# Packing the halves of Q and K without a DRAM buffer, and masks that stay on chip

## The reference

```python
def _L0_attn_ref(x, W_qkv, W_out, b_out):      # 16 heads of 32, WINDOW = 128
    qkv = jnp.einsum('ble,ef->blf', x, W_qkv).reshape(b, l, 16, 32, 3)
    q, k, v = ...                               # heads first
    q = q * cos + _rotate_half(q) * sin         # RoPE on neighbouring pairs
    k = k * cos + _rotate_half(k) * sin
    mask = (j <= i) & (j >= i - WINDOW)
    scores = jnp.where(mask, q @ k.T * 32 ** -0.5, finfo.min)
    out = softmax(scores) @ v
    return out.reshape(b, l, e) @ W_out + b_out

x = x + _layernorm(_L0_attn_ref(_layernorm(x), W_qkv, W_out, b_out))
x = x + _layernorm(_L0_ffn_ref(_layernorm(x), W_up, W_gate, W_down))   # ternary weights, SwiGLU, 512 -> 2048 -> 512
```

## Time and profile before

| what | us |
|---|---|
| median of 3 runs | 1574.02 (1569.62 to 1575.28) |
| the profiled execution, its own time | 1572.07 |
| its span, first to last instruction | 1570.3 |
| PE busy / DVE busy over the span | 1337.6 / 1078.8 |
| ACT busy / POOL busy over the span | 725.6 / 497.0 |
| first and last masking on DVE start at | 54.9 and 777.2 |

### The profile page before, as it was taken

The page is one execution under the profiler, slowest core; times in us unless marked ns, Lnnn a source line. Parts: engine busy times, 40 slices in busy tenths (PEclk is TensorE's granted clock), DMA queues, the critical chain, the costliest instruction groups (busy, mean ns, idle before and its releaser), DMA issues. The chain is left out here.

```text
span 1570.3 us, 23805 instructions
## 1 busy us (share of the span) xinstructions
PE 1337.6 (85%) x7942; PEld 732.5 (47%) x7942; DVE 1078.8 (69%) x2567; ACT 725.6 (46%) x1410; POOL 497.0 (32%) x594
## 2 busy tenths in 40 slices
PE   3678979988897897888540799999999999999995
PEld 2355646555564655555320344444444444444442
DVE  3678979888897888889729545646465555556553
ACT  1465766667666666756535223232322323232321
POOL 2535664655656456565320000102010101101011
PEclk9888989999998999999675899999999999999998
DMA  9588889889898879889834000000000000000000
GB/s 349 143 176 173 169 194 178 160 184 187 167 171 189 178 155 189 171 169 179 160 139 184 0 1 0 28 1 28 0 28 1 0 28 0 28 1 28 1 28 27
DMA packets 363769, 164.62 MB, mean 105 GB/s; under 512 B 293632, under 2 KB 348160, under 8 KB 362624
## 3 DMA queue, kind: packets, MB, share of 16 engines
q1 hardware_dynamic: 363648, 163.11, 46.1%
HBM read 64.42 MB, written 25.17 MB: 57 GB/s over the span
## 5 line engine op out<-in xcount | busy, mean ns | idle before, releaser
L587 ACT ACTIVATE prob<-prob,peak 128x256 f32<-128x256 f32 x512 | 230.6, 498 | 180.1 <-DVE peak L709 178.9
L883 PE MATMUL J<-xnT,weights 128*128 128x512 f32 x512 | 257.9, 630 | 7.9 <-ACT xnT L571 7.9
L709 DVE CUSTOM_DVE_ANT_0 prob<-S,band,neg_score_scale 128x256 f32<-128x256 f32 x512 | 226.4, 479 | 35.1 <-DMA band<-in_bands 23.8
L1127 DVE SCALAR_TENSOR_TENSOR su<-U,sig 128x512 f32<-128x512 f32 x128 | 88.5, 692 | 198.6 <-ACT sig L1063 196.8
L718 DVE SCALAR_TENSOR_TENSOR parts<-prob,parts 128x512 f16<-128x512 f32 x256 | 209.8, 820 | 19.3 <-ACT parts L595 19.1
L1063 ACT ACTIVATE sig<-U,sig_scale 128x512 f32<-128x512 f32 x128 | 88.1, 688 | 231.3 <-PE U L1205 231.3
L1205 PE MATMUL U<-xT_hi,up_q 128*128 128x512 f16 x512 | 194.6, 380 | 0.0
L1205 PE MATMUL U<-xT_lo,up_q 128*128 128x512 f16 x512 | 194.6, 380 | 0.0
L1216 PE MATMUL Y<-down_q,h_hi 128*128 128x512 fp8e4 x512 | 194.1, 379 | 0.5 <-DVE h_lo L1138 0.5
L1205 PE MATMUL G<-xT_hi,gate_q 128*128 128x512 f16 x512 | 194.0, 379 | 0.0
L1205 PE MATMUL G<-xT_lo,gate_q 128*128 128x512 f16 x512 | 194.0, 379 | 0.0
(11 more groups left out here) (122 smaller groups left out, 1980.6 us busy)
## 6 DMA issues: line engine op xcount, KB each, us to landing
spill<-split SPq DMA_DIRECT2D x64, 256.0 KB, 2.6
Qp<-spill SPq DMA_DIRECT2D x128, 128.0 KB, 2.8
Kp<-spill SPq DMA_DIRECT2D x128, 128.0 KB, 2.9
out_x<-o_sb SPq DMA_DIRECT2D x8, 1024.0 KB, 4.3
X<-in_x SPq DMA_DIRECT2D x1, 6144.0 KB, 25.7
weights<-parts SPq DMA_TRANSPOSE x256, 3.2
Kc<-Kp SPq DMA_DIRECT2D x32, 128.0 KB, 3.0
w_gate_here<-in_w_gate SPq DMA_DIRECT2D x2, 2048.0 KB, 9.7
```

The lines of the kernel that those rows point to most:

```text
L587: e = nc.scalar.activation(prob[:, u % 4, h, :], prob[:, u % 4, h, :], ACT.Exp, bias=peak[:, u % 4, h:h + 1], scale=-1.0)
L709: e = nc.vector.tensor_tensor_reduce(out=prob[:, u % 4, h, :], in0=S_ps[u % 2][:, h * 2 * P:(h + 1) * 2 * P], in1=(band0 if first_tile els ...
L883: e = pe.matmul(dst[:], W[:, s, c, g * P:(g + 1) * P], xnT[:, c, :], start=(c == 0), stop=(c == DC - 1))
L1127: nc.vector.scalar_tensor_tensor(su[:, c % 2, :], U_ps[c % 2][:], H_SCALE / XN_SCALE ** 2, sig[:, c % 2, :], ALU.mult, ALU.mult).then_inc( ...
```

## The change

- `spill_q`, `spill_k`, the DRAM buffer and its two semaphores go. `pack_q` and `pack_k` now read `split` in SBUF directly and wait for what the spill waited for (`r_lo_done`), beside their own waits. Their numbers, sizes and targets stay: four DMAs of 128 KB for each group.
- For that the rows of a group are in another order: dimension by dimension with the head innermost (row = 4 x dimension + head). The 128 rows of `split`, read in order, are then the 32 rows of a pack's target with four heads in each. The columns of the Q and K weights and the rows of the RoPE tables are permuted on the host, and the shuffle swaps rows 4 apart instead of 1.
- `moves` is shortened: packs stand at units 0 (K1), 5 (Q2), 6 (K2), 16 (Q3), 18 (K3), 24 (next Q0), 25 (next K0), 30 (next Q1). Before they stood at 1, 5, 8, 17, 19, 25, 26 and 31.
- `rotated_high` waits for the packs of the group before (64 for each group) where it waited for the spill (16).
- `band0` is loaded once and kept; `logits` takes it only for the first query tile of a batch and `band` otherwise. The load at unit 28 and its wait go; DVE waits once for it before its first work.

```diff
-        spill = nc.dram_tensor("spill", [2, 2, P, MT], F16).ap()
-            def spill_q(i, g):
-                n = i * NG + g
-                q_split, packed_before = worked_out(sp, 2 * n + 1, 64 * n)
-                sp.wait_ge(r_lo_done, q_split)
-                at_least(sp, q_packed, packed_before)
-                sp.dma_start(spill[0].rearrange("s p t -> p s t"), split[:, 0]).then_inc(q_spilled, 16)
             def pack_q(i, g):
                 n = i * NG + g
-                written, scored = worked_out(sp, 16 * (n + 1), (n - 1) * STEPS)
-                sp.wait_ge(q_spilled, written)
+                q_split, scored = worked_out(sp, 2 * n + 1, (n - 1) * STEPS)
+                sp.wait_ge(r_lo_done, q_split)
                 at_least(sp, score_done, scored)
                 for row, part in enumerate((0, 0, 1, 1)):
-                    sp.dma_start(Qp[row * HD:(row + 1) * HD, g % 2],
-                                 spill[0, part].rearrange("(h d) t -> d h t", h=4)).then_inc(q_packed, 16)
+                    sp.dma_start(Qp[row * HD:(row + 1) * HD, g % 2], split[:, 0, part]).then_inc(q_packed, 16)
...
-            moves = {0: [(spill_k, 1, 0)], 1: [(pack_k, 1, 0)],
-                     2: [(carry_k, 0, 0)], 4: [(spill_q, 2, 0)], 5: [(pack_q, 2, 0), (carry_v, 0, 0)],
-                     6: [(spill_k, 2, 0)], 8: [(pack_k, 2, 0)],
+            moves = {0: [(pack_k, 1, 0)],
+                     2: [(carry_k, 0, 0)], 5: [(pack_q, 2, 0), (carry_v, 0, 0)], 6: [(pack_k, 2, 0)],
                      10: [(carry_k, 1, 0)], 13: [(carry_v, 1, 0)],
-                     16: [(spill_q, 3, 0)], 17: [(pack_q, 3, 0)], 18: [(spill_k, 3, 0)], 19: [(pack_k, 3, 0)],
+                     16: [(pack_q, 3, 0)], 18: [(pack_k, 3, 0)],
                      20: [(carry_k, 2, 0)], 21: [(carry_v, 2, 0)],
-                     24: [(spill_q, 0, 1)], 25: [(spill_k, 0, 1), (pack_q, 0, 1)], 26: [(pack_k, 0, 1)],
+                     24: [(pack_q, 0, 1)], 25: [(pack_k, 0, 1)],
                      27: [(carry_k, 3, 0)], 29: [(carry_v, 3, 0)],
-                     30: [(spill_q, 1, 1)], 31: [(pack_q, 1, 1)]}
+                     30: [(pack_q, 1, 1)]}
...
-                    if plan is not LAST and u == 28:
-                        used, next_tile = worked_out(sp, i * UNITS + (NG - 1) * STEPS + 2, i + 1)
-                        sp.wait_ge(logit_done, used)
-                        sp.dma_start(band0[:], row(bands, next_tile)).then_inc(band0_in, 16)
...
-                at_least(act, (q_spilled, k_spilled)[a], 16 * n)
+                at_least(act, (q_packed, k_packed)[a], 64 * n)
...
-                                             [d ^ 1 for d in range(HD)]).then_inc(swap_done, 1)
+                                             [p ^ 4 for p in range(HD)]).then_inc(swap_done, 1)
...
-                if first_tile and u % 2 == 0:
-                    dve.wait_ge(band0_in, bands_in)
+                mask = band0 if first_tile and (i + u // UNITS) % PER_BATCH == 0 else band
...
-                        in1=(band0 if first_tile else band)[:], scale=neg_score_scale[:], scalar=3.0e38,
+                        in1=mask[:], scale=neg_score_scale[:], scalar=3.0e38,
```

More of the change, by code:

```diff
@@ L267, in attention @@
         const_in, bias_in, table_in, band0_in = sem("const_in"), sem("bias_in"), sem("table_in"), sem("band0_in")
-        q_spilled, k_spilled, q_packed, k_packed = sem("q_spilled"), sem("k_spilled"), sem("q_packed"), sem("k_packed")
+        q_packed, k_packed = sem("q_packed"), sem("k_packed")
         set_up, wmax_parts_done, wmax_done, wmax_spread, scales = (
@@ L332, in turn @@
                                        in_=parts[:, u % TURNED].rearrange("p s k -> p (s k)")).then_inc(p_turned[u % TURNED], 16)
-            def spill_q(i, g):
-                n = i * NG + g
-                q_split, packed_before = worked_out(sp, 2 * n + 1, 64 * n)
-                sp.wait_ge(r_lo_done, q_split)
-                at_least(sp, q_packed, packed_before)
-                sp.dma_start(spill[0].rearrange("s p t -> p s t"), split[:, 0]).then_inc(q_spilled, 16)
             def pack_q(i, g):
                 n = i * NG + g
-                written, scored = worked_out(sp, 16 * (n + 1), (n - 1) * STEPS)
-                sp.wait_ge(q_spilled, written)
+                q_split, scored = worked_out(sp, 2 * n + 1, (n - 1) * STEPS)
+                sp.wait_ge(r_lo_done, q_split)
                 at_least(sp, score_done, scored)
                 for row, part in enumerate((0, 0, 1, 1)):
-                    sp.dma_start(Qp[row * HD:(row + 1) * HD, g % 2],
-                                 spill[0, part].rearrange("(h d) t -> d h t", h=4)).then_inc(q_packed, 16)
[L350 to L355, removed]
+                    sp.dma_start(Qp[row * HD:(row + 1) * HD, g % 2], split[:, 0, part]).then_inc(q_packed, 16)
             def pack_k(i, g):
                 n = i * NG + g
-                written, scored, carried = worked_out(sp, 16 * (n + 1), (n - 1) * STEPS, 16 * (2 * i + g // 2))
-                sp.wait_ge(k_spilled, written)
+                k_split, scored, carried = worked_out(sp, 2 * n + 2, (n - 1) * STEPS, 16 * (2 * i + g // 2))
+                sp.wait_ge(r_lo_done, k_split)
                 at_least(sp, score_done, scored)
@@ L363, in pack_k @@
                 for row, part in enumerate((0, 1, 0, 1)):
-                    sp.dma_start(Kp[row * HD:(row + 1) * HD, g % 2],
-                                 spill[1, part].rearrange("(h d) t -> d h t", h=4)).then_inc(k_packed, 16)
+                    sp.dma_start(Kp[row * HD:(row + 1) * HD, g % 2], split[:, 1, part]).then_inc(k_packed, 16)
             def carry_k(i, g):
@@ L412, in row @@
                 return t[bass.ds(n, 1)].rearrange("a p k -> (a p) k")
-            spill_q(0, 0)
             pack_q(0, 0)
-            spill_k(0, 0)
             pack_k(0, 0)
-            spill_q(0, 1)
             pack_q(0, 1)
-            spill_k(0, 1)
             pack_k(0, 1)
@@ L700, in logits @@
                 first_tile = u // 2 % TT == 0
-                scored, halved, bands_in = worked_out(
-                    dve, i * UNITS + u + 1, i * UNITS + u - 3, 16 * (i + 1 + u // UNITS))
+                scored, halved = worked_out(dve, i * UNITS + u + 1, i * UNITS + u - 3)
                 settled(dve, x0_in)
@@ L798, in _ @@
             dve.wait_ge(bias_in, 16)
+            dve.wait_ge(band0_in, 16)
             dve.wait_ge(set_up, 5)
@@ L1357, in by_tile @@
     def by_tile(t):
-        t = np.tile(t.T.astype(np.float32), (P // HD, 1))
+        t = np.repeat(t.T.astype(np.float32), P // HD, axis=0)
         t = t.reshape(P, PER_BATCH, MT).transpose(1, 0, 2)
@@ L1369, in band_masks @@
     seen = (k >= q) & (k <= q + WINDOW)
-    masks = np.zeros((NM, P, 2 * P), np.float32)
-    for i in range(NM):
-        masks[i][~(seen & ((k >= P) | (i % PER_BATCH != 0)))] = NEG
+    masks = np.zeros((2, P, 2 * P), np.float32)
+    for i in range(2):
+        masks[i][~(seen & ((k >= P) | (i != 0)))] = NEG
     return masks
@@ L1380 @@
     cos_t, sin_t = rope_tables()
+    w_qkv = np.asarray(L0_attn_W_qkv).reshape(D, NG, 4, HD, 3)
+    w_qk = [w_qkv[..., part].transpose(0, 1, 3, 2).reshape(D, D) for part in range(2)]
     arrays = {
         "x": np.ascontiguousarray(L0_attn_x),
-        "w_qkv": np.ascontiguousarray(np.asarray(L0_attn_W_qkv).reshape(D, D, 3).transpose(2, 0, 1)),
+        "w_qkv": np.ascontiguousarray(np.stack([*w_qk, w_qkv[..., 2].reshape(D, D)])),
         "w_out": np.ascontiguousarray(L0_attn_W_out),
```

## The result

| kernel | us, median | runs, range |
|---|---|---|
| before | 1573.49 | 7, 1569.62 to 1578.22 |
| after | 1586.58 | 7, 1583.86 to 1595.34 |

The ratio is 1.0088, with an interval of 1.0063 to 1.0112: the change makes the kernel 13.9 us slower (0.0088 x 1573.5), where the prediction had 1536 and a range up to 1558.

What follows compares the result with a forecast made beforehand. The prediction took DVE's in-order stream, waits included, to bound attention. Masks 23, RoPE tables 11 and start 2.8 made 36.8 us off the profiled 1572.1, 1535.3, adjusted towards the median to 1536; range 1512 to 1558 us.

Steps and rivals of the forecast that it cites:

- the same issue time and the same landing: SP's packs: reading SBUF instead of DRAM changes neither; bounds 0.3 us per group of packs, 4 us in all either way.
- Kc<-Kp: Profile row of an SBUF-to-SBUF DMA with 512 short pieces, landing in 3.0 us; taken as nearest guide from above for packs.
- 14 places: The 7 tile boundaries and 7 RoPE places for which a changed pack cost was counted, 4 us either way.
- DVE's in-order stream: Attention: DVE's work with its waits sets a tile's length; PE's waits on transposes are slack in most places.
- The masks: DVE's first-tile masking: resident masks remove 23 of 23.8 us of waits; bounds 0 and 23.8.
- the tables: DVE's wait before Q's RoPE product: cosT and sinT issued 2.2 us sooner save 11 of 15.2 us; bounds 0 and 15.2.
- rival (a): SP's queue: its relief counts too, half of PE's 59.5 us of transpose waits comes through, 1506 us; chance 0.12.
- The start: Before the first exp: K packs begin 4.8 us sooner, ACT's high half limits the gain to 2.8; bounds 0 and 4.8.
- rival (d): ACT's high half of third Q and K waits for late SBUF packs; decides from 7.2 us landing; 1589 us, chance 0.05.
- The slots: SP's queue: transposes behind moved packs go up to 0.7 us later or 1 to 2.6 sooner; costed at nothing, 17 us if wrong.
- (c): Attention: no gain, DVE's freed time turns up in its wait on PE's weighted values; 1566 to 1574 us, chance 0.06.
- The signs: Wrong if DVE's waits on weighted values grow over 10 us, ACT's high half waits on a DMA, or packs land after 4 us.

Runs made afterwards that it cites:

- e6_dram_1kb: The kernel after, but packs read a DRAM buffer written once at the start, in 1 KB pieces, no spills in the loop (output wrong): 1542.97 us, 0.9816.
- e1_masks: The kernel before with the two masks resident and nothing else changed; packs still go through DRAM: 1573.77 us, 1.0003.
- v3_masks_tables: The kernel before with the masks resident and the RoPE tables loaded at unit 17 instead of 19: 1579.77 us, 1.0027.
- e2_packs: The kernel after with the mask reload and its wait put back; packs read SBUF directly: 1597.34 us, 1.0154.
- e5_old_slots: The kernel after with its packs back in the units they had before: 1597.93 us, 1.0136.
- e4_dram_source: The kernel after, but packs read a DRAM buffer written once at the start, in 4 KB pieces, no spills in the loop (output wrong): 1541.51 us, 0.9808.
- e7_stay_in_32: The kernel after, but each pack reads a constant SBUF row on its target's own 32 partitions, four times (scores wrong): 1559.90 us, 0.9932.
- e9_dram_reload: e6_dram_1kb with the mask load at unit 28 and its wait put back (output wrong): 1547.92 us, 0.9858.
- e11_q_on_act: The kernel after with Q's packs issued from ACT's queue instead of SP's, at units 6, 16, 24 and 30: 1575.73 us, 1.0008.
- v1_fewer_packs: Packs through DRAM as before, but five pack DMAs per group of Q and K instead of eight; masks resident, tables at unit 17: 1587.96 us, 1.0102.
- v2_act_spills: v3_masks_tables with the 64 spills issued by ACT, one unit behind its high half, and one pack a unit earlier: 1565.33 us, 0.9923.
- v4_pool_spills: v2_act_spills, but POOL issues the spills, right behind its low half: 1579.35 us, 1.0040.
- v5_act_q_packs: v2_act_spills, but ACT issues Q's packs as well as the spills: 1578.39 us, 1.0033.
- probe_burst: No layer computed: only bursts of four 128 KB copies from DRAM or SBUF, with and without a transpose behind; landings 2.6 us from DRAM, 3.2 from 128 partitions onto 32.

## Why the prediction was wrong

**The step that failed.** "I take the same issue time and the same landing; the bounds are 0.3 us faster and 0.3 us slower for each group of packs". This term was mis-sized. A group of four packs costs SP 0.7 us more (4 x 0.17) and each of the DMA engines 1.4 us more ((778 - 689) / 64), and lands 0.8 (Q) to 1.4 us (K) later. By e6_dram_1kb against after, the source alone is 43 us, where the bounds allowed 4. The nearest row taken, Kc<-Kp with 3.0 us, was no guide: it has many short pieces, but it does not gather 128 partitions into 32. The price was also set for only 14 places on the assumed path, while 64 groups pass through the queue and the DMA engines that PE's transposes need.

**The premise behind it.** "I therefore take DVE's in-order stream, with these waits in it, as what sets a tile's length; PE's waits on transposes are slack in most places." This fell too. The masks, priced at 23 us, gave 0 on the kernel before (e1_masks), 7 with the relieved queue and 10 on the packs from SBUF; the tables, priced at 11, gave nothing (v3_masks_tables). The rows that said so were there: 59.5 us of PE on transposes, and the prediction had even set rival (a) on them, with half of the 59.5.

What follows the span best is PE's idle time before two kinds of matmul, the weighted values, which need a transpose, and the scores, which need the packs. Both wait for DMAs in SP's queue. The table adds all lines of PE's waits before them, whoever ended them, from 0 to 860 us. For the scores the largest lines are, before and after:

```profile
PE S L835 <- issue: 21.0, 12, 4.3
```
```profile
PE S L806 <- DMA Kp<-split: 5.1, 1, 5.1
```

| kernel | weighted values | scores | sum | span |
|---|---|---|---|---|
| before | 64.8 | 35.0 | 99.8 | 1570.3 |
| after | 99.5 | 12.0 | 111.5 | 1582.1 |
| e1_masks | 63.3 | 39.0 | 102.3 | 1575.8 |
| e2_packs | 106.1 | 14.7 | 120.8 | 1596.1 |
| e5_old_slots | 73.8 | 47.5 | 121.3 | 1595.8 |
| e4_dram_source | 53.0 | 12.4 | 65.4 | 1537.4 |
| e6_dram_1kb | 54.7 | 13.5 | 68.2 | 1541.7 |
| e7_stay_in_32 | 77.6 | 15.7 | 93.3 | 1561.4 |
| e9_dram_reload | 56.9 | 14.2 | 71.1 | 1542.5 |
| e11_q_on_act | 91.2 | 13.1 | 104.3 | 1574.1 |
| v1_fewer_packs | 71.1 | 45.6 | 116.7 | 1587.8 |
| v2_act_spills | 54.7 | 30.6 | 85.3 | 1554.1 |
| v3_masks_tables | 63.5 | 50.3 | 113.8 | 1581.7 |
| v4_pool_spills | 60.7 | 45.4 | 106.1 | 1578.8 |
| v5_act_q_packs | 65.5 | 27.4 | 92.9 | 1575.1 |

Against before, the sum moves as the span does, within 5 us, in every kernel but v5_act_q_packs, where it is 12 us off. The change did what it was meant to do for the scores, 23 us less, and lost 35 before the weighted values. Exchanging the source alone (e6_dram_1kb to after) puts 45 us on the weighted values and takes 2 off the scores. This is an account of where the time lies, not a proof of what sets it: as PE's busy time hardly changes (1336.8 us in after, 1329.2 in e6_dram_1kb), a longer launch must show up as idle time of PE somewhere. My reading is that a tile's length is set by the ring from DVE's low half through SP's transpose to PE's weighted values and back to DVE, and by the packs where they come late, and that the waits on mask and tables were time that DVE had in hand. Fewer issues on SP do not by themselves make a faster kernel: v1_fewer_packs, v4_pool_spills (both beside v3_masks_tables) and v5_act_q_packs (beside v2_act_spills) have them and gained nothing.

**The start** was right in sign: the first exp at 51.55 instead of 55.88, 4.3 us sooner, where 2.8 were forecast. But ACT's high half did wait for packs there, as rival (d) has it (timeline of after):

```profile
46.46 0.63 ACT L553 ACTIVATE split<-rot 128x512 f16<-128x512 f32 x1 [6.30 <-DMA Qp<-split]
...
49.82 0.63 ACT L553 ACTIVATE split<-rot 128x512 f16<-128x512 f32 x1 [2.73 <-DMA Kp<-split]
...
51.55 1.72 ACT L559 ACTIVATE prob<-prob,peak 128x256 f32<-128x256 f32 x4 [1.10 <-DVE peak L679]
```

**The slots.** Moving transposes behind packs a unit up or down was "cost at nothing"; e5_old_slots shows that the earlier packs are worth 8 us, in favour, with the SBUF source, and the table shows where: before the scores.

**The rivals.** (d) named the cause, packs from SBUF that land late, with a chance of 0.05, but put it at ACT's high half with 7.2 us as the point from which it decides. ACT's waits on packs after are only 9.0 us in 2 times; the place is SP's queue and the DMA engines, in front of the transposes, and there 3.6 and 4.3 us decide. (c) said that DVE's freed time turns up in its wait on PE's weighted values. It does turn up in e1_masks, but mostly behind ACT; in after, DVE waits for PE 42.6 us instead of 25.3. (a), the queue's relief, is real as well: e9_dram_reload has it without the masks, 22 us together with the slots and the spills' bytes. What the change does is then: relief and slots -22, masks -7, source +43, together +14. These are successive differences, so that they add up proves nothing, and the 7 is hardly larger than its doubt. The largest, the source, was changed by itself.

**The signs** named in advance did their work: DVE's waits on PE's weighted values grew by 17 us (10 was the limit), packs of K took 4.3 us (4 was the limit), and ACT's high half waited on a DMA. The tiles did not come closer together: from the first masking of tile 0 to that of tile 7 they are 91.6 us apart before and 93.6 after, where about 87 was forecast. The mask wait gone, the RoPE wait halved and the early first exp came as forecast; the launch was not shortened by them.

## What to carry to other kernels

A wait that is long in the table is worth removing only if the engine behind it is what the rest waits for: add up all waits of that engine before and after, and where the sum does not fall, look for the engine whose waits moved with the time. Where a queue issues time-critical transfers in order, price every other DMA by its issue time and its use of the DMA engines, not by whether its own landing is awaited; a transfer behind or beside a transpose can delay it as one ahead of it does. Here packs read from DRAM were cheaper than a direct SBUF-to-SBUF transfer that gathers 128 partitions into 32; measure such a shape first, and beside the traffic it will have.

## What the runs showed of the hardware

- A DMA of 128 KB in pieces of 1 KB took SP 0.43 us to issue from DRAM and 0.60 from SBUF, and landed, in bursts by itself, in 2.6 us from DRAM, 2.1 within 128 partitions, 2.4 within 32, and 3.2 from 128 partitions onto 32. With a transpose behind each of six bursts, the last kept the DMA engines busy for 28.2 us where the one from DRAM took 20.3; without transposes it was 14.5 and 11.3.
- Packets of 256 bytes of a DMA transpose took 34 ns in the mean beside copies from 128 partitions onto 32, and 21 to 23 beside the other three kinds (probe_burst).
- Four such packs ahead of a transpose in SP's queue held it for 3.74 us in the place shown. Issued from ACT, the Q packs took 5.1 us to land instead of 3.6 (e11_q_on_act).
- Fewer bytes did not mean less DMA time: 145.41 MB took 778 us of each engine and 163.11 MB took 724.
